# One of 32 row gathers of a graph kernel, fetched row by row from SyncE and ScalarE

## The reference

```python
h_fwd = h @ W_forward.T
h_rev = h @ W_reverse.T
messages = h_fwd[src] * direction[:, 0:1] + h_rev[src] * direction[:, 1:2]
scores = leaky_relu(einsum('ef,hf->eh', messages, attn_forward[0]), 0.2)
exp_scores = exp(scores - scores.max(axis=0, keepdims=True))
sum_exp = segment_sum(exp_scores, dst)
norm = exp_scores / (sum_exp[dst] + 1e-10)
outs = [segment_sum(messages * norm[:, hd:hd + 1], dst) for hd in range(4)]
```

## Time and profile before

| | us |
|---|---|
| median of 3 executions | 2908.91 |
| their lowest and highest | 2907.92 and 2914.72 |
| the profiled execution, its own time | 2913.43 |
| its span, first to last instruction | 2911.7 |
| edge loop, SyncE's first loop instruction to ScalarE's last chunk | 101.3 to 2046.8 |

### The profile page before, as it was taken

The page is one execution under the profiler, slowest core; times in us unless marked ns, Lnnn a source line. Parts: engine busy times, 40 slices in busy tenths (PEclk is TensorE's granted clock), DMA queues, the critical chain, the costliest instruction groups (busy, mean ns, idle before and its releaser), DMA issues. The chain is left out here.

```text
span 2911.7 us, 37450 instructions
## 1 busy us (share of the span) xinstructions
PE 996.6 (34%) x5889; PEld 785.7 (27%) x5890; DVE 1130.0 (39%) x3750; ACT 748.8 (26%) x2810; POOL 1802.5 (62%) x1908
## 2 busy tenths in 40 slices
PE   5312112121211121121112111211462889999800
PEld 5212111111211121121111111211452555656500
DVE  6533333333333333333333333333574222222287
ACT  4222222222222222222222222222351223333321
POOL 3677777777777777777777777777175112222257
PEclk9555555555555555555555555555555999999955
DMA  5222222222222222222222222222254652222264
GB/s 167 55 57 57 57 57 57 58 57 57 57 58 57 57 57 57 57 57 58 57 57 57 58 57 57 57 58 56 66 183 161 191 171 81 82 82 83 73 206 150
DMA packets 186477, 235.78 MB, mean 81 GB/s; under 512 B 63048, under 2 KB 150515, under 8 KB 186080
## 3 DMA queue, kind: packets, MB, share of 16 engines
q0 software_dynamic: 59872, 135.00, 17.2%
q1 hardware_dynamic: 90000, 67.70, 7.7%
q10 hardware_dynamic: 36336, 30.80, 4.2%
HBM read 182.75 MB, written 45.06 MB: 78 GB/s over the span
## 5 line engine op out<-in xcount | busy, mean ns | idle before, releaser
L185 POOL DMA_INDIRECT rows<-node_table,index x1568 | 1482.1, 945 | 535.7 <-issue 472.6
L598 PE MATMUL p_win<-hot_ex,msg 128*65 128x64 f32 x3136 | 393.7, 319 | 1558.2 <-DVE hot_ex L710 1278.1
L598 PEld LDWEIGHTS p_win<-hot_ex,msg 128*65 128x65 f32 x3136 | 359.5, 229 | 1592.3 <-issue 1295.6
L633 ACT ACTIVATE p_part<-rows,attr_all 128x64 f32<-128x64 f32 x1568 | 388.4, 299 | 1437.8 <-DMA rows<-node_table,index 1437.8
L679 DVE TENSOR_TENSOR part<-rows,p_attr 128x544 f32<-128x544 f32 x196 | 141.4, 721 | 869.6 <-DMA rows<-node_table,index 550.9
L1307 POOL DMA_INDIRECT expert_rows<-ys,back x104 | 101.2, 973 | 420.6 <-DVE ys L1452 414.9
L672 DVE TENSOR_TENSOR acc<-acc,p_win 65x64 f32 x784 | 171.0, 218 | 393.6 <-issue 312.9
L1410 PE MATMUL p_y<-w_sb,hid_t 128*128 x832 | 200.5, 384 | 1.4 <-ACT hid_t L1337 1.4
L1395 PE MATMUL p_h<-w_sb,xt 128*128 x416 | 199.2, 602 | 0.3 <-issue 0.3
L1337 ACT ACTIVATE hid_t<-p_ht,b_sb 128x128 f32<-128x128 f32 x416 | 118.9, 368 | 273.6 <-DVE ys L1452 107.2
L1436 DVE COPY hid<-p_h 128x512 f32<-128x512 f32 x104 | 71.9, 692 | 243.2 <-PE p_h L1395 243.2
(11 more groups left out here) (225 smaller groups left out, 1200.2 us busy)
## 6 DMA issues: line engine op xcount, KB each, us to landing
rows<-node_table,index POOLq DMA_INDIRECT x1568, 2.5
w_sb<-in_w SPq DMA_DIRECT2D x32, 512.0 KB, 4.2
xs<-dispatched ACTq DMA_DIRECT2D x104, 129.0 KB, 2.1
b_t<-in_b ACTq DMA_DIRECT2D x104, 128.0 KB, 3.1
y<-expert_rows SPq DMA_DIRECT2D x12, 896.0 KB, 10.7
token_rows<-in_x SPq DMA_DIRECT2D x7, 896.0 KB, 5.4
residual<-x SPq DMA_DIRECT2D x7, 896.0 KB, 6.0
token_rows<-xn SPq DMA_DIRECT2D x7, 896.0 KB, 4.8
```

What stands on the lines that cost most here:

```text
L185: pool.indirect_dma_start(out=rows[:, s, k, :], out_offset=None, in_=table, in_offset=bass.IndirectOffsetOnAxis(ap=index[:, s, k:k + 1], a ...
L598: last = pe.matmul(psum[0:MSG, u * HEADS * W:(u + 1) * HEADS * W], msg[:, v, k, :], weighted[:, k, :, :].rearrange("p h w -> p (h w)"), st ...
L633: last = act.activation(p_part[:, v, k, :], rows[:, s, k, COLS:COLS + HD], ACT.Copy, scale=attr_all[:, 1, ds(c * K + k, 1)])
```

## The change

GpSimd no longer gathers the eighth row set (`k = 7`) of slot 3. In each iteration, the 128 rows that this gather brought are fetched by 128 separate DMAs: 48 from ScalarE (16 after each of three chunks) and 80 from SyncE (32, 24 and 24). Each of these copies one table row of 544 bytes to one partition, as two pieces of 272 bytes, from a row address held in a register. Four row numbers at a time are taken to registers by `load`. The numbers come from a new array `src_rows` (prepared on the host, 49 x 128) through a new tile `row_index`, one partition wide, which SyncE loads once per iteration.

Both engines start the rows of iteration `it` once all chunks of the former iteration have used theirs (`rows_used` and `rev_part` at `it * RING`). ScalarE and VectorE wait, before slot 3, for the seven gathers and for both new counts (`all_gathered`). SyncE's index loads now stand behind its rows, and each waits for the gathers of its slot. SyncE reloads `row_index` after its own last load from it and after ScalarE has signalled `act_indices`. ScalarE's order in an iteration: chunk 0, rows 16 to 31, chunk 1, rows 32 to 47, chunk 2, chunk 3, rows 0 to 15 of the next iteration.

```diff
+BY_ACT = 16
+BY_SP = (32, 24, 24)
...
         def gather(pool, s):
-            for k in range(K):
+            for k in range(K if s < RING - 1 else K - 1):
...
                     for s in range(RING):
                         sp.dma_start(index[:, s, :], src[s]).then_inc(index_ready[s], 16)
+                    sp.dma_start(row_index[:, :], src_rows[0:1, :]).then_inc(row_index_ready, 16)
...
+            def rows_one_by_one(eng, it, first, n, done):
+
+                eng.wait_ge(row_index_ready, 16 * (it + 1))
+                settle(eng, row_turns)
+                for p in range(first, first + n, 4):
+                    loaded = load(eng, row_index[:, p:p + 4], NP - 1)
+                    for q in range(4):
+                        eng.dma_start(rows[p + q:p + q + 1, RING - 1, K - 1, :].rearrange("p (a c) -> p a c", a=2),
+                                      table[ds(loaded[q], 1), :].rearrange("r (a c) -> r a c", a=2)).then_inc(done, 16)
+
+            def all_gathered(eng, s, it):
+
+                n = K if s < RING - 1 else K - 1
+                eng.wait_ge(gathered[s], 16 * n * (it + 1))
+                if s == RING - 1:
+                    eng.wait_ge(rows_by_sp, 16 * sum(BY_SP) * (it + 1))
+                    eng.wait_ge(rows_by_act, 16 * 3 * BY_ACT * (it + 1))
...
                 def _(sp):
-                    def step(c, s, it, _):
-                        after(sp, gathered[s], 16 * K * it)
+                    def next_index(c, s, it):
+                        sp.wait_ge(gathered[s], 16 * (K if s < RING - 1 else K - 1) * (it + 1))
                         sp.dma_start(index[:, s, :], src[c] if isinstance(c, int)
                                      else src[ds(c, 1)].rearrange("a p k -> (a p) k")).then_inc(index_ready[s], 16)
...
+                    def step(c, s, it, ahead):
+
+                        if s == 0:
+                            after(sp, rows_used, it * RING)
+                            after(sp, rev_part, it * RING)
+                        if s < RING - 1:
+                            rows_one_by_one(sp, it, 3 * BY_ACT + sum(BY_SP[:s]), BY_SP[s], rows_by_sp)
+                        if not ahead:
+                            return
+                        if s == RING - 1:
+                            sp.wait_ge(act_indices, it + 1)
+                            settle(sp, row_turns)
+                            sp.dma_start(row_index[:, :], src_rows[it + 1:it + 2, :] if isinstance(it, int) else
+                                         src_rows[ds(it + 1, 1), :]).then_inc(row_index_ready, 16)
+                        next_index(c + RING, s, it)
...
-                        act.wait_ge(gathered[s], 16 * K * (it + 1))
+                        all_gathered(act, s, it)
...
+                        if s < RING - 2:
+                            single_rows(it, s + 1)
+                        if s == RING - 1 and not (isinstance(it, int) and it == NIT - 1):
+                            single_rows(it + 1, 0)
+
+                    def single_rows(it, q):
+                        if q == 0:
+                            act.wait_ge(rows_used, it * RING)
+                            act.wait_ge(rev_part, it * RING)
+                        rows_one_by_one(act, it, q * BY_ACT, BY_ACT, rows_by_act)
+                        if q == 2:
+                            act.sem_inc(act_indices, 1)
...
-                        dve.wait_ge(gathered[s], 16 * K * (it + 1))
+                        all_gathered(dve, s, it)
...
+        "src_rows": src[RING - 1::RING, :, K - 1],
```

More of the change, by code:

```diff
@@ L44 @@
 EARLY = 2
+BY_ACT = 16
+BY_SP = (32, 24, 24)
+assert 3 * BY_ACT + sum(BY_SP) == P and RING == 4
 NCH = -(-EDGES // (CHUNK * RING)) * RING
@@ L117, in alternate, with build @@
     step(NG - 1, 0, NG // 2)
-def build(nc, x, src, dst, attr, w_fwd, w_rev, w_fwd_t, w_rev_t, attn_t, gate_w, gate_b,
+def build(nc, x, src, src_rows, dst, attr, w_fwd, w_rev, w_fwd_t, w_rev_t, attn_t, gate_w, gate_b,
           w1, b1, w2, b2, gamma, beta, out):
@@ L164, in stage_edges @@
 def stage_edges(nc, tensors, g):
-    x, src, dst, attr, table, dispatched = (g[n] for n in ("x", "src", "dst", "attr", "table", "dispatched"))
+    x, src, src_rows, dst, attr, table, dispatched = (g[n] for n in ("x", "src", "src_rows", "dst", "attr", "table", "dispatched"))
     ident, ones, eps, iota_w, token_rows, acc, run_max, neg_shift = (
@@ L180, in stage_edges @@
         gathered = [esem(f"gathered{s}") for s in range(RING)]
+        row_index = esb("row_index", [1, P], I32)
+        row_index_ready = esem("row_index_ready")
         def gather(pool, s):
-            for k in range(K):
+            for k in range(K if s < RING - 1 else K - 1):
                 pool.indirect_dma_start(out=rows[:, s, k, :], out_offset=None, in_=table,
@@ L559, in stage_edges @@
             turns = sem("pool_turns")
+            rows_by_sp = sem("rows_gathered_by_sp")
+            rows_by_act = sem("rows_gathered_by_act")
+            row_turns = sem("row_turns")
+            act_indices = sem("act_row_indices_taken")
             rows_used = sem("rows_used")
@@ L605, in _ @@
                 def _(sp):
-                    def step(c, s, it, _):
-                        after(sp, gathered[s], 16 * K * it)
+                    def next_index(c, s, it):
+                        sp.wait_ge(gathered[s], 16 * (K if s < RING - 1 else K - 1) * (it + 1))
                         sp.dma_start(index[:, s, :], src[c] if isinstance(c, int)
                                      else src[ds(c, 1)].rearrange("a p k -> (a p) k")).then_inc(index_ready[s], 16)
-                    chunks(sp, lambda it: None, step, RING)
+                    def step(c, s, it, ahead):
[12 more added lines that the diff above has]
+                        next_index(c + RING, s, it)
+                    for s in range(RING):
+                        step(s, s, 0, True)
+                    with sp.Fori(1, NIT - 1) as it:
+                        for s in range(RING):
+                            step(it * RING + s, s, it, True)
+                    for s in range(RING):
+                        step((NIT - 1) * RING + s, s, NIT - 1, False)
                 @block.gpsimd
@@ L639, in step @@
                            .then_inc(exp_ready, 1)
-                    chunks(act, lambda it: None, step)
+                        if s < RING - 2:
[9 more added lines that the diff above has]
+                            act.sem_inc(act_indices, 1)
+                    rows_one_by_one(act, 0, 0, BY_ACT, rows_by_act)
+                    for s in range(RING):
+                        step(s, s, 0, None)
+                    with act.Fori(1, NIT - 1) as it:
+                        for s in range(RING):
+                            step(it * RING + s, s, it, None)
+                    for s in range(RING):
+                        step((NIT - 1) * RING + s, s, NIT - 1, None)
                 @block.tensor
```

## The result

| | before | after |
|---|---|---|
| median, us | 2908.97 | 4588.71 |
| lowest and highest | 2907.92 and 2914.72 | 4588.08 and 4590.33 |
| span of the profiled execution | 2911.7 | 4587.5 |
| iteration of the edge loop | 40.0 | 74.2 |

The account below looks back on a forecast made before the run. GpSimd's gather issue bounded the kernel before; SyncE would bound it after. Block start 101.3 us, 49 x 74.7 = 3660 and 46 branches x 3.7 = 170 put ScalarE's last chunk at 3932, 1885 later: 4795 us stated, range 4350 to 5350.

Parts of the forecast that it names:

- SyncE becomes the bound, the rest is hidden: Edge loop: SyncE's 80 rows and index loads take 71.2 us per iteration; GpSimd's 38.75 and ScalarE's 54 fit beneath.
- The gain of 61 us for GpSimd: Edge loop: one gather in 32 removed, 1.25 us per iteration, 61 us in all if GpSimd stays the bound.
- The piece, 3.51 us: SyncE's load of four row numbers plus four one-row DMAs, taken from the `pad_row` stores, less 0.15 us for the load.
- a transfer of another partition count saves nothing: Issue time of a one-row DMA: no faster than a 128-row one, so 0.33 us was taken.
- the main forecast: Edge loop bound by SyncE at 0.25 to 0.45 us per issue, total about 4400 to 5250 us; 73%.
- Landing and use, W + 3.45: After SyncE's work W per iteration: last row lands, ScalarE runs eight activations, two semaphore hops; 3.45 us until SyncE may restart.
- The branch: SyncE's loop end: a long body of 350 instructions costs 3.5 us before the next instruction, as on VectorE.
- the second hole: SyncE's first load after the loop branch: some 2.1 us lost inside it, as seen on VectorE.
- The sum: Looped SyncE iteration of 71.2 + 5.1 + 2.1 = 78.4 us; over the kernel 1885 us added, 4795 us stated.
- a nearly free issue: Rival for one-row DMAs: issue of 0.05 us, looped iteration 56.0 us, total about 3695 us; 8% for 3600 to 4350.
- contention of the two engines: Rival: ScalarE's 48 issues hold SyncE up, 16 us per iteration, 780 more, 5575 us; 14% for more than 5250.
- the arrival of the gain: Rival: both engines fetch their rows within 38.75 us, GpSimd stays the bound, 2848 us; 4%.

## Why the prediction was right, and where it was off

- **SyncE becomes the bound, the rest is hidden:** shown. The wait ahead of slot 3 names the rows, ScalarE's rows left out change nothing, and SyncE's halved rows give back 970 us. ScalarE's own iteration, put at 54 us, lasted 54.35 once it was the bound.
- **The gain of 61 us for GpSimd:** 58 measured with the rows left out.
- **The piece, 3.51 us:** 3.36 measured in the first set (25.04 us, less 1.5 for the last four issues, over seven pieces); the median of all pieces on SyncE is 3.31, from load to load. Two errors cancelled in part. One is the issue: 0.228 us, not 0.33, and 0.42 from one to the next, not 0.52. The step "a transfer of another partition count saves nothing" leaned on 106 rows against 128, and one row is outside of that. A single-partition transfer of the same program, `row_index`, issued in 0.237 us. Whether it is the one partition or the few pieces that makes it quick is open: nothing was measured between 8 pieces and 128. The other error is the TENSOR_LOAD: 0.55 us, not 0.34. I corrected `pad_row`'s 0.497 downward by the loads of VectorE and TensorE, which are other engines and do not follow a DMA issue on their own engine. The first load of an iteration on SyncE, not behind a row's issue, and the register instructions after it:

```profile
L600 SPq FUSED_REGOPS  x4: 147/150/159, 1061.6 to 1063.5; - x4
L600 SPq SEQ_ASSERT  x4: 18/18/24, 1062.9 to 1063.7; - x4
L600 SPq TENSOR_LOAD <-row_index x1: 469/469/469, 1061.1 to 1061.1; - x1
```

  So 0.13 of the 0.21 us is there without a row's issue ahead, and the uncorrected row of the same engine was the better guide.
- **Luck in the number:** the main forecast asked for 0.25 to 0.45 us per issue, and 0.228 is below that. By the prediction's own sum the cheaper issues alone would have brought the time to some 4400 us (80 x 0.1 x 49 = 392 less), the dearer loads alone to some 5000 (20 x 0.21 x 49 = 206 more). These are estimates. That 4589 came out nearer to 4795 than the issue deserved is the second error making up for the first.
- **Landing and use, W + 3.45:** the last row's issue begins at 1056.10 and ScalarE's eight activations at 1057.57, 1.5 us; 1.6 was charged, and 0.1 for the semaphore, which no row had shown.
- **The branch:** 2.7 us, 3.5 charged; the second hole, behind the first register operation of the load (the lines above), about 1.0 us, 2.1 charged.
- **The sum:** charged 71.2 + 5.1 + 2.1 = 78.4 us. Measured, from the end of a set's last row at 1056.3: 4.8 to the next load (1061.1), 1.0 for the second hole, 68.4 for the rest, 74.2. The difference of 4.2 us is 2.8 in the pieces, 0.3 and 1.1 in the holes; times 49 it is 206 us, which is what 4795 exceeds 4589 by.
- **The rivals:** a nearly free issue did not come true, though the issue was a third cheaper than taken; contention of the two engines is refuted, by one execution and its trace; the arrival of the gain would have needed 1.7 us per piece. The rule of the Trainium skill behind it (DMA: Bandwidth & Descriptors, Issuing engines are not separate DMA queues) calls the time to initiate a DMA usually small relative to the DMA. Here the sequencer spends 0.84 us per row, issue and share of the load, on 544 bytes, and from the start of the last issue to the first use of its row it is 1.5 us. Rows can be under way together, but SyncE's share follows one upon the other 80 times: for such a size the trace decides the other way.

## What to carry to other kernels

An engine without a line on the page of busy times is not free: ask for its queue, and multiply its instructions. Before work is handed to it, find the same sequence on the same engine elsewhere in the trace, add up whole pieces with register loads, range checks and gaps, and compare them with the time that one loop iteration leaves, for each engine that takes a share. If the sum is above that, make the piece cheaper and do it less often. Without range checks, and with the rows of every second iteration only, a loss of 1680 us became a gain of 33; leaving out the checks alone had left a loss of 520.

## What the runs showed that I had not expected

- The gaps between register instructions count too: removing eight instructions that last 0.68 us took 1.07 us off a piece, so 0.05 us of gap went with each.
- Issues of one-partition DMAs follow one another every 0.41 us ((9.76 - 0.23) / 23), of which 0.228 is the issue itself.
- The same program can take 2915 or 4379 us, and the kernel before 2916 or 3495, in sets on different chips. Each set's own runs of the kernel before showed it at once; the cause was not found.
